# An MoE layer's list stage: SyncE's wait for an add's landing, moved behind the next turning

## The chip, the cores and the metric

The kernel runs on one core of a Trainium2 chip. The metric is the device time of one execution in microseconds (us), the median of the runs. Engines are called PE (TensorE, matmuls; PEld its weight loads), DVE (VectorE), ACT (ScalarE), POOL (GpSimd) and SP (SyncE).

## What is computed

Eight batches of 512 tokens of width 512 pass a cross-attention block and a feed-forward block, each behind a layer norm and with a residual:

```python
x = x + xattn(layernorm(x), ctx_512, Wq, Wkv_expand, Wout)      # 16 heads, 64 context rows
x = x + ffn(layernorm(x), ...)
# ffn, for T = 4096 tokens, E = 8 experts, I = 256:
scores, top_idx = top_k(x @ router_w.T, 2)
comb = zeros((T, E)).at[arange(T)[:, None], top_idx].set(scores)
h = silu(einsum('td,edi->eti', x, wg)) * einsum('td,edi->eti', x, wu)
moe_out = einsum('etd,te->td', einsum('eti,eid->etd', h, wd), comb)
se = silu(x @ sg_w + sg_b) * (x @ su_w + su_b) @ sd_w + sd_b
out = moe_out + se
```

## The kernel before

Tokens are worked in 32 tiles of 128. A first part does attention and the router tile by tile. Then comes one list of 103 entries that share one pipeline: 32 entries of the shared expert, and behind them SLOTS = 71 slots of the routed experts. A slot is up to 128 (token, expert) pairs of one expert; slots are sorted by expert, so there are seven places where the expert changes. "Slot t" below is entry 32 + t, and the change touches only the slots.

What one slot does, engine by engine:

- POOL gathers its token rows from DRAM into one of four buffers (`gather(t)`, line 722, a DMA from POOL's queue), and, much later, adds its result rows onto `out` in DRAM (`add(t)`, line 732, also a DMA of POOL's queue, which accumulates). POOL's own order is gather(t), add(t-6), gather(t+1), add(t-5), and so on.
- PE turns the gathered rows (line 1447, four transposes), one entry later does gate and up (line 1456, 12 matmuls), and two entries after that the down product (line 1456, 6 matmuls that read `hidT`). In one PE entry the order is: transposes of slot t, gate and up of slot t-1, down of slot t-3.
- ACT and DVE form `hid` = silu(gate)*up (lines 925 and 1421), then split it into a high and a low f16 part in `xn2p` (lines 752 and 1385; two buffers). This is "the split activations".
- SP turns the split activations: `turn_hid(t)`, line 517, one DMA transpose from `xn2p` into one of the four buffers of `hidT`. It waits for the split of slot t. PE's down product of slot t waits for its landing. Below this is "turning t".
- DVE scales the down product into one of four buffers of y (line 1436; the tile is named `w_q` in the rows), and POOL's add(t) reads that.

Two adds of different experts can hit the same token, so the add of a slot that begins a new expert must not start before the one ahead of it has landed; within an expert it is enough that the adds up to t-3 have (and by POOL's own wait, t-2). POOL does not decide this itself. SP does, in `pass_turn(t)`: it loads a number that was computed from the routing (line 522), waits until the landed adds have raised their semaphore to it (line 523; the rows show the end of that wait at line 524), and raises `add_turn` (line 524). POOL's add(t) waits for `add_turn` to reach t-2. From slot 3 on there is one such step a slot. As SP runs its list in order, a `turn_hid` that stands behind a waiting `pass_turn` waits too.

```python
def pass_turn(t):
    before_t = sp.value_load(adds_before[0:1, t - 1:t], min_val=16, max_val=16 * SLOTS)
    sp.wait_ge(y_added[(t - 1) % 2], before_t)
    sp.sem_inc(add_turn, 1)

def add(t):                                   # POOL
    pool.wait_ge(y_ready, T + t + 1)
    wait(pool, y_added[t % 2], 16 * (t // 2))
    ...
    wait(pool, add_turn, t - 2)
```

Of the kernel before, what the change touches and what calls it, by code (L numbers as in the profile page):

```python
# [44 lines left out]
SLOTS = 2 * T + E - 1  # L45
# [45 lines left out]
def xattn_moe(nc, x, ctxT, wqT, wkT, wvT, woT, routerT, experts, shared, sh_b, sd_b, out):  # L91
# [5 lines left out]
    with stack:  # L97
# [274 lines left out]
        def _(sp):  # L372
# [141 lines left out]
            def turn_hid(t):  # L514
                sp.wait_ge(parts_ready, t + 1)
                wait(sp, down_mm, T + t - 3)
                sp.dma_start_transpose(hidT[:, t % 4, :, :, :].rearrange("p v c q -> p (v c) q"),
                                       hid_parts[:, t % 2, :, :].rearrange("p v i -> p (v i)")
                                       ).then_inc(hid_turned[t % 4], 16)

            def pass_turn(t):
                before_t = sp.value_load(adds_before[0:1, t - 1:t], min_val=16, max_val=16 * SLOTS)
                sp.wait_ge(y_added[(t - 1) % 2], before_t)
                sp.sem_inc(add_turn, 1)

            for t in range(SLOTS + 1):
                if t < SLOTS - 1:
                    turn_hid(t)
                if t >= 4:
                    pass_turn(t - 1)  # L530


        @block.gpsimd
# [398 lines left out]
        def _(dve):  # L932
# [93 lines left out]
            def low_values(n):  # L1026
                for i, ((rows, dst, src), (_, high, _)) in enumerate(zip(value_parts(1, n), value_parts(0, n))):
                    dve.wait_ge(v_hi, 2 * n + i + 1)
                    low(dst, src, sc[rows, S_V:S_V + 1], high, v_split)
# [718 lines left out]
```

## Time and profile before

| | us |
|---|---|
| median of 3 runs | 790.71 (790.65 to 793.01) |
| the profiled execution, its time | 791.66 |
| its span in the trace | 789.9 |
| PE busy | 760.1 (96%) |
| DVE, ACT, POOL busy | 579.8, 460.0, 433.8 |
| granted TensorE clock, mean | 0.997 |

The span is what the trace covers of one execution; 1.8 us of the execution's time lie around it. PE's busy share says that it is the engine that works nearly all the time. The chain of work that ended last is the place where a wait shows that lengthened the run, and the stretch of the slots begins at about 461 us and ends at 779.7 us, the last down product.

### The profile page before, as it was taken

Reading aid. Unit: us, or ns where it says so; the run is one execution under the profiler, and the core shown is the slowest. Engines: PE = TensorE matmul, PEld = TensorE weight load, DVE = VectorE, ACT = ScalarE, POOL = GpSimd, SP = SyncE. Lnnn points to the kernel's source line nnn. Section 1 sums busy time; section 2 is a strip of 40 time slices with the busy share of each in tenths; the row PEclk is TensorE's granted clock in tenths of the full one; section 3 lists DMA queues with packets and bytes.
Section 4 is the critical chain, followed back from the end, with each engine's and each line's share of the span. In section 5 each row is a group of like instructions: output and inputs, shape, how many; then the busy total and the mean of one; then the engine's idle time right before and its main releaser. Section 6 shows DMA issues by size and latency. Waiting matters only on the chain.

```text
span 789.9 us, 21975 instructions
## 1 busy us (share of the span) xinstructions
PE 760.1 (96%) x7252; PEld 520.8 (66%) x7252; DVE 579.8 (73%) x1199; ACT 460.0 (58%) x847; POOL 433.8 (55%) x563
## 2 busy tenths in 40 slices
PE   5898999999999999999999999999999999999995
PEld 2767888888888887778888864455554545455552
DVE  5999999999989898856898765555555555565552
ACT  4688888998898989775556333333333333333330
POOL 2455787777777777552200203756565565656543
PEclk9999999999999999999999999999999999999998
DMA  8326867777676777778666646989898888979992
GB/s 293 125 78 182 230 192 223 214 211 212 197 217 200 217 220 215 202 221 264 209 201 202 227 137 124 163 136 161 140 156 140 149 144 152 147 134 163 145 148 34
DMA packets 138319, 140.73 MB, mean 178 GB/s; under 512 B 87872, under 2 KB 88896, under 8 KB 137856
## 3 DMA queue, kind: packets, MB, share of 16 engines
q1 hardware_dynamic: 122336, 104.01, 48.6%
q0 software_dynamic: 15904, 35.70, 26.0%
q8 instruction: 47, 0.77, 0.4%
q14 instruction: 32, 0.26, 0.1%
HBM read 71.61 MB, written 52.31 MB: 157 GB/s over the span
## 4 chain that ended last, share of the span: by engine, by line
PE 84%; DVE 7%; DMA 5%; issue 2%; ACT 1%; POOL 0%; SPq 0%; DVEq 0%; POOLq 0%; ACTq 0%
PE psum L1456 45%; PE psum L1525 19%; PE psum L1447 10%; PE psum L1575 5%; DMA hidT<-xn2p 4%; PE psum L1618 3%; DVE kv_store L974 1%; DMA out<-w_q,tabs 1%; DVE head_max L1162 1%; DVE stats L1078 1%; PE psum L1504 1%; DVE probsT L974 1%; DVE w_q L1436 0%; DVE attnT L1132 0%; DVE xn1T L974 0%
## 5 line engine op out<-in xcount | busy, mean ns | idle before, releaser
L732 POOL DMA_INDIRECT out<-w_q,tabs x71 | 112.5, 1584 | 110.7 <-DVE w_q L1436 80.5
L722 POOL DMA_INDIRECT x_in<-normed_tokens,tabs x71 | 71.4, 1006 | 89.9 <-DVE tabs L1315 42.2
L925 ACT ACTIVATE silu_g<-psum,tabs 128x256 f32<-128x256 f32 x71 | 33.6, 473 | 146.0 <-PE psum L1456 143.9
L1421 DVE SCALAR_TENSOR_TENSOR hid<-psum,tabs,silu_g 128x256 f32<-128x256 f32 x71 | 34.3, 484 | 111.2 <-ACT silu_g L925 108.1
L1456 PE MATMUL psum<-exp_all,hidT 128*128 x426 | 103.4, 379 | 3.2 <-DMA hidT<-xn2p 3.2
L1456 PE MATMUL psum<-exp_all,probsT 128*128 x420 | 96.4, 379 | 0.0
L1525 PE MATMUL psum<-xn1T,w_q 128*128 128x128 f16 x1536 | 91.0, 219 | 0.8 <-DVE maxima L957 0.8
L1456 PE MATMUL psum<-w_o,attnT 128*128 128x512 f16 x384 | 88.0, 379 | 1.7 <-DVE attnT L1132 1.3
L1525 PEld LDWEIGHTS psum<-xn1T,w_q 128*128 128x128 f16 x1536 | 86.3, 98 | 2.1 <-issue 2.1
L574 POOL TENSOR_TENSOR exp_all<-piece,exp_all 128x512 f32 (+1 forms) x48 | 56.0, 1166 | 44.5 <-ACT piece L752 44.5
L1456 PEld LDWEIGHTS psum<-exp_all,hidT 128*128 128x128 f16 x426 | 41.7, 98 | 54.2 <-issue 6.2
L1436 DVE TENSOR_SCALAR w_q<-psum,y_w 128x512 f32<-128x512 f32 x71 | 53.3, 751 | 22.1 <-PE psum L1456 17.6
L1456 PEld LDWEIGHTS psum<-exp_all,probsT 128*128 128x128 f16 x420 | 41.1, 98 | 41.9
L1456 PEld LDWEIGHTS psum<-w_o,attnT 128*128 128x128 f16 x384 | 35.1, 97 | 40.9 <-issue 1.6
L752 ACT ACTIVATE probsT<-psum 128x512 f16<-128x512 f32 x99 | 55.6, 600 | 9.0 <-PE psum L1447 8.5
L752 ACT ACTIVATE xn2p<-hid 128x256 f16<-128x256 f32 x70 | 29.2, 417 | 38.6 <-DVE hid L1421 36.4
L1456 PE MATMUL psum<-exp_all,xn1T 128*128 x216 | 49.6, 379 | 0.0
L1456 PE MATMUL psum<-exp_all,qT 128*128 x216 | 49.6, 379 | 0.0
L1575 PE MATMUL psum<-kv_store,qT 128*128 128x256 f16 x384 | 48.5, 273 | 0.2 <-DVE qT L974 0.2
L1456 PE MATMUL psum<-w_sh,hidT 128*128 128x512 f16 x192 | 46.7, 379 | 0.1
L646 POOL TENSOR_TENSOR xn2p<-xn,xn2p 128x512 f16<-128x512 f32 x32 | 37.1, 1159 | 17.4 <-ACT xn2p L752 15.4
L1525 PE MATMUL psum<-probsT,w_sh 128*128 128x128 f16 x768 | 45.5, 219 | 0.0
(216 smaller groups left out, 1652.0 us busy)
## 6 DMA issues: line engine op xcount, KB each, us to landing
x_in<-x SPq DMA_DIRECT2D x64, 256.0 KB, 3.1
exp_all<-experts SPq DMA_DIRECT2D x24, 512.0 KB, 5.2
out<-xy SPq DMA_DIRECT2D x32, 256.0 KB, 3.2
normed_tokens<-xn SPq DMA_DIRECT2D x32, 256.0 KB, 5.2
normed_turned<-xn2T SPq DMA_DIRECT2D x32, 256.0 KB, 3.4
w_q<-out SPq DMA_DIRECT2D x32, 256.0 KB, 2.9
out<-w_q SPq DMA_DIRECT2D x32, 256.0 KB, 2.1
probsT<-normed_turned SPq DMA_DIRECT2D x16, 256.0 KB, 3.5
```

Of the source, the lines that this page charges most:

```text
L574: pool.tensor_tensor(split_piece(e, 1, k), piece[:, :], split_piece(e, 0, k), ALU.subtract).then_inc(piece_split, 1)
L646: pool.tensor_tensor(xn2p[:, 1, :], xn2[:, (j + 1) % 2, 0:H], xn2p[:, 0, :], ALU.subtract).then_inc(xn2_parts, 1)
L722: pool.indirect_dma_start(x_in[:, t % 4, :], None, xn_dram, bass.IndirectOffsetOnAxis(gather_at[:, t:t + 1], 0)).then_inc(gathered[t % 4], 16)
L732: pool.indirect_dma_start(out, bass.IndirectOffsetOnAxis(add_at[:, t:t + 1], 0), y[:, t % Y_RING, :], None, bounds_check=TOKENS - 1, oob_i ...
L752: act.activation(dst, src, ACT.Copy, scale=scale).then_inc(done, 1)
L925: act.activation(silu_g[:, :], psum[:, GU_BANK[m % 2], 0:I], ACT.Silu, scale=gate_scale_at[:, tm:tm + 1]).then_inc(silu_ready, 1)
L1421: dve.scalar_tensor_tensor(hid[:, :], psum[:, GU_BANK[m % 2], I:2 * I], up_scale_at[:, tm:tm + 1], silu_g[:, :], ALU.mult, ALU.mult).then_ ...
L1436: dve.tensor_scalar(y[:, k % Y_RING, :], bank(DOWN_BANK[k % 2]), y_w[:, tk % 4, :], None, ALU.mult).then_inc(y_ready, 1)
L1447: last = pe.transpose(dst[:, c * P:(c + 1) * P], src[:, c * P:(c + 1) * P], ident[:, :])
L1456: last = pe.matmul(dst, lhsT(a, c), rhs(z, c), start=(c == 0 and a == z == 0), stop=(c == n - 1 and a == 1))
L1525: last = pe.matmul(dst[:, o * P:(o + 1) * P], weights(a, c, o), xT[:, z, c, :], start=(c == 0 and a == z == 0), stop=(c == C - 1 and a == 1))
L1575: last = pe.matmul(dst, qT[:, a, c, :], k_bd[:, z, c, :, :].rearrange("p h k -> p (h k)"), start=(a == z == 0 and (j != 2 or c % 2 == 0)), ...
```

## The change

The loop of SP that does both jobs for the slots is run one step longer, and the step that lets an add go is done one turn later. Before, SP's order was turning t, then pass_turn(t-1). Now it is turning t, then pass_turn(t-2).

```diff
-            for t in range(SLOTS + 1):
+            for t in range(SLOTS + 2):
                 if t < SLOTS - 1:
                     turn_hid(t)
-                if t >= 4:
-                    pass_turn(t - 1)
+                if t >= 5:
+                    pass_turn(t - 2)
```

SP's list at the head of the slots, before. L517 is a turning, L522 the load of `adds_before` that opens a pass_turn; a wait for `y_added` belongs to the pass_turn ahead of the row at which it is printed. The five turnings are 0 to 4, the first load is pass_turn(3).

```order
L517 DMA_TRANSPOSE hidT<-xn2p 128x4x128 [waits down_mm,parts_ready,adds_ready]
L517 DMA_TRANSPOSE hidT<-xn2p 128x4x128 [waits down_mm,parts_ready] x4
L522 TENSOR_LOAD adds_before
L522 ISA x2
L517 DMA_TRANSPOSE hidT<-xn2p 128x4x128 [waits y_added0,down_mm,parts_ready]
L522 TENSOR_LOAD adds_before
```

The same place of the changed kernel:

```order
L517 DMA_TRANSPOSE hidT<-xn2p 128x4x128 [waits down_mm,parts_ready] x5
L522 TENSOR_LOAD adds_before
L522 ISA x2
L517 DMA_TRANSPOSE hidT<-xn2p 128x4x128 [waits y_added0,down_mm,parts_ready]
L522 TENSOR_LOAD adds_before
```

One more turning (number 5) stands ahead of the first pass_turn; from there on the two alternate as before, with the slot numbers of pass_turn one lower against those of the turnings.

SP's list at the end of the slots, before. The last turning is number 69; behind it stand pass_turn(68), (69) and (70).

```order
504 L517 DMA_TRANSPOSE hidT<-xn2p 128x4x128 [waits y_added0,down_mm,parts_ready]
505 L522 TENSOR_LOAD adds_before
506 L522 ISA x2
507 L522 TENSOR_LOAD adds_before [waits y_added1]
508 L522 ISA x2
509 L522 TENSOR_LOAD adds_before [waits y_added0]
510 L522 ISA x2
511 L97 UNCONDITIONAL_BRANCH [waits y_added1]
```

And of the changed kernel:

```order
501 L517 DMA_TRANSPOSE hidT<-xn2p 128x4x128 [waits y_added1,down_mm,parts_ready]
502 L522 TENSOR_LOAD adds_before
503 L522 ISA x2
504 L522 TENSOR_LOAD adds_before [waits y_added0]
505 L522 ISA x2
506 L522 TENSOR_LOAD adds_before [waits y_added1]
507 L522 ISA x2
508 L522 TENSOR_LOAD adds_before [waits y_added0]
509 L522 ISA x2
```

Four instead of three pass_turn steps stand behind the last turning, pass_turn(67) to (70). The instructions of PE, DVE, ACT and POOL are the same, in the same order.

## Rows read from the trace of the kernel before

**Rows 1.** The page: the chain that ended last by engine.

```profile
PE 84%; DVE 7%; DMA 5%; issue 2%; ACT 1%; POOL 0%; SPq 0%; DVEq 0%; POOLq 0%; ACTq 0%
```

**Rows 2.** The waits, 395 to 790 us: waiter, releaser; us, times, longest.

```profile
PE psum L1456 <- DMA hidT<-xn2p: 3.2, 5, 1.0
SPq L524 <- DMA out<-w_q,tabs: 22.8, 8, 3.9
```

**Rows 3.** The chain in order of time, same stretch: start us, us, what.

```profile
502.15 0.44 PE psum L1447 x4
...
592.91 0.44 PE psum L1447 x4
...
598.38 7.07 DMA hidT<-xn2p
...
674.35 6.55 DMA hidT<-xn2p
...
769.03 0.44 PE psum L1447 x4
```

**Rows 4.** The timeline, 559 to 575 us: start us, us, engine line [idle before <-releaser].

```profile
561.97 0.99 POOL L722 DMA_INDIRECT x_in<-normed_tokens,tabs  x1 [0.30 <-issue]
...
563.37 0.41 DVE L1385 TENSOR_TENSOR xn2p<-hid,xn2p 128x256 f16<-128x256 f32 x1
...
564.28 1.59 POOL L732 DMA_INDIRECT out<-w_q,tabs  x1 [1.32 <-DVE w_q L1436]
...
569.84 1.46 PE L1456 MATMUL psum<-exp_all,hidT 128*128 x6
...
571.14 0.60 PE L1447 MATMUL psum<-ident,x_in 128*128 128x128 f32 x4
```

**Rows 5.** SP by line, ns min/median/max, first and last start: 517, then 524 from 563 us.

```profile
L517 SPq DMA_TRANSPOSE hidT<-xn2p x70: 1189/1190/2506, 475.4 to 774.5; - x70
...
L524 SPq EVENT_SEMAPHORE  x1: 17/17/17, 565.8 to 565.8; - x1
```

**Rows 6.** An expert's change, 590 to 606 us: POOL's timeline, SP's line 524, PE.

```profile
590.21 1.59 POOL L732 DMA_INDIRECT out<-w_q,tabs  x1 [1.44 <-DVE w_q L1436]
...
596.27 1.59 POOL L732 DMA_INDIRECT out<-w_q,tabs  x1 [3.19 <-SPq L524]
...
599.51 1.59 POOL L732 DMA_INDIRECT out<-w_q,tabs  x1 [0.30 <-issue]
...
L524 SPq EVENT_SEMAPHORE  x1: 17/17/17, 595.3 to 595.3; - x1
```

**Rows 7.** DMA queues, 559.49 to 561.6 us: packets, MB, share of 16 engines.

```profile
q1 hardware_dynamic: 544, 0.13, 30.8%
```

**Rows 8.** The same, 598.38 to 600.4 us.

```profile
q0 software_dynamic: 130, 0.25, 103.7%
q1 hardware_dynamic: 18, 0.00, 1.2%
```

**Rows 9.** The same, 498.46 to 503.3 us.

```profile
q1 hardware_dynamic: 544, 0.13, 26.2%
```

**Rows 10.** The timeline, 486 to 503 us.

```profile
495.93 0.99 POOL L722 DMA_INDIRECT x_in<-normed_tokens,tabs  x1 [0.30 <-SPq L524]
497.22 1.59 POOL L732 DMA_INDIRECT out<-w_q,tabs  x1 [0.30 <-issue]
498.02 0.41 DVE L1385 TENSOR_TENSOR xn2p<-hid,xn2p 128x256 f16<-128x256 f32 x1
499.11 0.99 POOL L722 DMA_INDIRECT x_in<-normed_tokens,tabs  x1 [0.30 <-issue]
```

**Rows 11.** The end: the chain, and POOL's timeline from 764 us.

```profile
774.92 6.59 DMA out<-w_q,tabs x2
...
778.81 1.55 POOL L732 DMA_INDIRECT out<-w_q,tabs  x1 [2.33 <-DMA out<-w_q,tabs]
...
782.52 1.55 POOL L732 DMA_INDIRECT out<-w_q,tabs  x1 [0.30 <-issue]
```

## The prediction

> **What bounds the kernel now.** Start with the chain that ended last [rows 1]: 84% of it is PE, so the run is PE working without a break, and only what makes PE wait or what comes behind PE's last product can move the time. The second view is the chain in order of time for the slots [rows 3]. Slot 9's transposes start at 502.15 us and slot 30's at 592.91, so 21 slots took 90.76 us, or 4.322 each. From slot 30 to slot 70 (769.03) it is 176.12 us for 40 slots, where 40 x 4.322 = 172.87. **3.25 us** were lost there. The chain names the place: three pieces "DMA hidT<-xn2p" of 6.5 to 7.07 us, of which the rows show the first and the last, are turnings that landed after PE wanted them, and the waits list five such waits, 3.2 us in all [rows 2]. The rest of the 3.25 us follows directly behind each, as PE catches up with the engines it feeds. One of the five is at the start of the slots and outside the stretch.
>
> The third view is one undisturbed slot [rows 4]. DVE ends the split of slot 21 at 563.78 and SP issues turning 21 at once (563.81). Its down product starts at 569.84. A turning has thus **6.03 us** to land: two periods, 8.64 us, less 2.61. How much it needs is seen in the DMA queues. A turning is 544 packets of queue 1, and for turning 20 all 544 lie within 2.1 us of the issue [rows 7].
>
> Why was turning 29 late, which was issued on time at 598.38? SP waited for the landing of add 25 (issued 590.21, released at 595.3, so 5.1 us) before it could issue turning 28, and let add 26 go only then, at 596.27 instead of some 594.5 [rows 6]. Turning 28 had slack for its 1.4 us. But add 26, the gather behind it and add 27 (599.51) now sat on the DMA engines at the wrong moment: in the first 2.0 us of turning 29, queue 0 filled the engines (103.7%) and only 18 of the 544 packets moved [rows 8]. So what costs PE time is not SP's wait as such, but **where an add's transfer lies against a turning**. SP's waits for adds were 22.8 us in 8 pieces [rows 2] and cost PE 3.25.
>
> **The change, step by step.**
>
> *In every slot, SP's step comes later.* SP reaches line 524 some 2.0 us after it issued the turning (563.81 to 565.8), 1.19 of them the issue itself [rows 5], and POOL's add starts 1.0 us behind line 524 (595.3 to 596.27, [rows 6]). Before, add t was let go behind turning t+1, long ahead of its data: add 19 waited only for DVE and started at 564.28, that is 0.5 us behind turning 21 [rows 4]. Now add t is let go behind turning t+2, so it starts at 2.0 + 1.0 = 2.9 to 3.0 us behind turning t+2. Every add, and with it every gather in POOL's order, moves **2.4 us** later within a period of 4.32. The add then stands 1.4 us ahead of the next turning, where it stood 3.8 ahead.
>
> *At a change of expert, SP no longer holds a turning back.* Add t-1 starts 2.9 behind turning t+1 and lands 5.1 later, which is 3.7 behind turning t+2. The next turning is due at 4.32. SP waits some 1.7 us in idle time. The three late pieces should go: **-3.25 us**, taken whole. If an add needs over 5.8 us, part of this stays.
>
> *Turnings against the shifted adds.* This is the unknown. The best row is at the start of the slots, where the queue happened to stand nearly as it will in every slot: turning 6 was issued at 498.43 (the end of its split), with an add 1.2 us ahead (497.22) and a gather 0.7 behind (499.11) [rows 10]. After the change the figures are 1.4 ahead and 0.5 behind. All 544 packets were through within 4.8 us [rows 9], against 2.1 for turning 20, and PE was not held up by it. With 6.03 us to land in, that holds, with about 1 us to spare. The row at the other side is turning 29, with its add 2.1 ahead: 7.07 us, too late. Bounds: nothing from turning 6; from the 6.55 us of the milder late piece in [rows 3], a period of (6.55 + 2.61) / 2 = 4.58, so 0.26 us on some 62 slots, **+16 us**. I take **+1.0**, three or four late landings of some 0.3 us, as 1.4 is nearer to 1.2 than to 2.1. It can't be below nothing, as PE has no other gap.
>
> The Trainium skill, in "DMA: Bandwidth & Descriptors", section "Queues, rings and completion order", says that each DMA engine round-robins between its queue rows packet by packet. By that rule a turning should get its share while an add runs, and a shifted add would cost it little: the term above would be 0 and the sum 1.0 us lower. [Rows 8] speak against leaning on it here, with 18 packets of one queue beside 130 of the other.
>
> *Gathers come later.* Gather 25 starts at 561.97 and its transposes at 571.14, 9.2 us behind [rows 4]; 2.4 less leaves 6.8. At a change the add is released by a landing at 3.7, starts at 4.6 to 4.7 instead of 2.9, and takes the gather behind it along: 5.1 us are left. No row gives a gather's landing. The shortest margin that the trace shows is gather 9, 495.93 [rows 10], with transposes at 502.15 [rows 3]: 6.2 us, and PE did not wait. So the ordinary slots are covered by 0.6, and the changes are not shown to be. Bounds: 0, and 5 changes x 1.5 = 7.5 us, if a gather needs the 6.55 of the slowest turnings. I take 0.2 at each of the five changes whose add lands slowly, **+1.0**.
>
> *The y buffers* (four) are no limit: add t-4 starts 2.9 us behind turning t-2 and lands 5.1 later, at 8.0; DVE writes the y of slot t some 14.7 behind it at the earliest (two periods and 6.03 to the down product).
>
> *The end.* The last turning (69) is issued at 774.5 [rows 5]. Behind it, before, only pass_turn(68) to (70) stand, which hold nothing up: add 67 goes at 774.92 with its data, add 68 at 778.81, add 70 at 782.52 [rows 11]. Now pass_turn(67) stands there too, so add 67 starts at 774.5 + 3.0 = 777.5, 2.6 us later. Add 69 must wait for its landing, by POOL's own wait; an add took 5.1 us in traffic, and at the end add 68 took 2.7 (778.81 to the end of the chain's piece at 781.51). With 4.2 between them, add 69 may start at 777.5 + 4.2 + 1.0 = 782.7 and add 70 one instruction and gap (1.55 + 0.3) later, at 784.6: **+2.1 us**, and nothing hides it, since PE is done by then. With 2.7 for the landing it is +0.6, with 5.1 it is +3.0.
>
> *Sum* against the profiled execution's 791.66: -3.25 + 1.0 + 1.0 + 2.1 = +0.85, so 792.5. The median is 0.95 below the profiled execution, which gives **791.6**.
>
> **The rivals.**
>
> *A. The shifted adds make turnings late all the time: slower.* The mechanism is that of turning 29, in every slot. It decides at 6.03 us between a turning's issue and its landing. For it: an add 2.1 us ahead cost 7.07, turning 6 had only about 1 us of slack, and a stalled PE widens the period, which moves the add from 1.4 ahead towards 2.1. Against it: turning 6, and that no second add follows closely, as add 27 did. A third of the 16 us is 5.3 us; with the other terms (-3.25 + 1.0 + 2.1) that is +5.2, and the median **796**. Two late gathers of over 1 us have the same sign.
>
> *B. The gain without the costs: faster.* Turnings and gathers all land in time and the end costs only its lower bound: -3.25 + 0.6 = -2.65, **788.1**. For it: the three late pieces are a clear loss, and the tail's price hangs on one landing. It needs everything at its lower end.
>
> *C. The change does not take the wait away.* If adds at the changes take 6 us in the new traffic, SP still holds turnings back, and half of the 3.25 us stays: **793.2**. In sign it lies with the forecast or with A.
>
> **How the numbers follow.** About 0.3%, 2.4 us, is what a measurement of this kernel can tell from no change. The forecast (both small terms together under 2.5 us) has 0.48, A has 0.34, B 0.08, C 0.10, of which 0.02 lie inside 2.4 us. So faster 0.08, same 0.50, slower 0.42. The range reaches down to 788.8, into B, and up to 798.5, past A's 796 but far from the 16 us bound.
>
> **What the new profile would show.** POOL's adds (line 732) each wait for SP's line 524 and start 2.9 us behind a turning. The waits of SPq L524 for "DMA out" are then short and no turning starts late. The three late pieces of 6.5 us and more are gone from the chain, and transposes come every 4.32 us. Where A holds, "DMA hidT<-xn2p" stands in the chain slot after slot, and the period is above 4.32. Where gathers are late, PE's line 1447 waits for "DMA x_in" a few slots behind each change. The last add starts some 15.6 us behind slot 70's transposes, not 13.5 (769.03 to 782.52). The prediction is wrong if the period changes at all outside the changes of expert, or if the end does not move.

## The result and the profile after

The changed kernel takes **798.71 us** (median of 6 runs, 798.28 to 800.96), the kernel before beside it 791.12 us (6 runs, 790.52 to 793.12). The ratio is 1.0097, with a 95% interval of 1.0076 to 1.0117: slower by 7.6 us. The forecast was 791.6, "same"; the range ended at 798.5, just below the measured time. Ratios here and below leave out four executions that stand far above the others of their kernel (805.14 us with the old end, 2046.42 with the gathers ahead, 816.91 and 818.97 with known turns). The profiled execution took 798.28 us with a span of 796.6; that of before took 791.66.

First the page of the changed kernel: the chain by engine (before: [rows 1]), and POOL's adds, whose columns are busy us, mean ns, idle before them and what ended most of it.

```profile
PE 81%; DVE 6%; issue 4%; DMA 4%; SPq 2%; ACT 1%; POOL 1%; POOLq 0%; DVEq 0%; ACTq 0%
...
L732 POOL DMA_INDIRECT out<-w_q,tabs x71 | 112.8, 1589 | 115.9 <-SPq L524 77.5
```

PE's share fell from 84 to 81%: PE waits more. Next the waits behind 395 us (waiter, releaser; us, times, longest), to be set beside [rows 2]:

```profile
POOL out L732 <- SPq L524: 77.5, 41, 3.3
POOL out L732 <- DVE w_q L1436: 18.8, 7, 3.7
PEld psum L1456 <- issue: 7.5, 8, 2.1
PEld psum L1447 <- issue: 4.2, 8, 0.8
PE psum L1456 <- DMA hidT<-xn2p: 4.1, 3, 1.9
PEld psum L1447 <- DMA x_in<-normed_tokens,tabs: 3.9, 5, 1.7
PE psum L1447 <- DMA x_in<-normed_tokens,tabs: 1.8, 2, 1.2
```

and SP's own wait in the same stretch:

```profile
SPq L524 <- DMA out<-w_q,tabs: 13.8, 9, 2.9
```

The adds now wait for SP, as the change intends. SP's waits for adds shrank from 22.8 to 13.8 us. Waits of the transposes (line 1447) for gathers, "DMA x_in", are new against the first trace of before. Then the chain in order of time (start us, us, what), to be set beside [rows 3] and [rows 11]; slot 9's transposes are at 504.87 and slot 30's at 596.82:

```profile
491.01 7.47 DMA hidT<-xn2p
...
504.87 0.44 PE psum L1447 x4
...
596.82 0.63 PE psum L1447 x4
...
640.58 4.78 DMA x_in<-normed_tokens,tabs
...
679.93 6.29 DMA x_in<-normed_tokens,tabs
...
773.77 0.44 PE psum L1447 x4
...
779.24 1.19 SPq L517
...
782.53 4.83 DMA out<-w_q,tabs x2
787.74 1.42 issue
789.15 1.55 POOL out L732
```

The three late turnings between slots 30 and 70 are gone from the chain. Two late gathers stand there instead, and the end is another. PE's transposes cut the executions into stretches. The columns are us; "slot 0" is where its transposes start, "product 70" is the start of slot 70's down product, and "again" is the second trace of the same kernel, from the experiments below:

| kernel | slot 0 at | slots 0 to 9 | 9 to 30 | 30 to 70 | slot 70 to product 70 | to the end |
|---|---|---|---|---|---|---|
| before | 460.94 | 41.05 | 90.75 | 176.12 | 9.79 | 11.28 |
| after | 462.76 | 41.95 | 92.11 | 176.79 | 11.80 | 11.15 |
| difference | +1.82 | +0.90 | +1.36 | +0.67 | +2.01 | -0.13 |
| before, again | 463.51 | 40.18 | 90.81 | 174.25 | 9.79 | 11.28 |
| after, again | 461.74 | 41.70 | 92.06 | 176.38 | 11.40 | 11.44 |

The 1.82 us ahead of the slots, where the change touches nothing, are chance: over all kernels of this study slot 0 starts between 460.3 and 463.5 us, and in the second pair of traces it is the kernel before that starts later. One piece of it may be a stretch of 3.4 us from 24.4 us at a granted clock of 0.5 (1.2 GHz; PE had been busy for 2.6 of the 4.4 us ahead of it), which the first execution of before didn't have and the second did. From slot 0 on the changed kernel is 4.8 us longer in the first pair of traces and 6.7 in the second.

Does the adds' shift have the size that was predicted? POOL's timeline shows an ordinary slot (start us, us, engine line, operation, [idle before <- releaser]); the turning of the slot was issued at 668.93:

```profile
668.93 18.49 SPq L517 DMA_TRANSPOSE hidT<-xn2p  x5
...
669.74 0.99 POOL L722 DMA_INDIRECT x_in<-normed_tokens,tabs  x1 [0.31 <-issue]
...
672.30 1.59 POOL L732 DMA_INDIRECT out<-w_q,tabs  x1 [1.57 <-SPq L524]
...
676.26 0.60 PE L1447 MATMUL psum<-ident,x_in 128*128 128x128 f32 x4
```

The add starts 3.4 us behind the turning, which is also the median over adds 10 to 64, where 2.9 to 3.0 was predicted. The gather has 6.5 us to its transposes (median; before 9.3).

### The profile page after: what moved, and what is told of

It reads as the page before. It is cut to its first block, busy times and chain, and to the rows that moved or that the text cites. A ratio compares the mean times of both kernels' runs of the same rounds, so it can differ in the third digit from the quotient of the medians.

```text
span 796.6 us, 21975 instructions
## 1 busy us (share of the span) xinstructions
PE 761.9 (96%) x7252; PEld 520.6 (65%) x7252; DVE 580.4 (73%) x1199; ACT 460.1 (58%) x847; POOL 432.9 (54%) x563
## 4 chain that ended last, share of the span: by engine, by line
PE 81%; DVE 6%; issue 4%; DMA 4%; SPq 2%; ACT 1%; POOL 1%; POOLq 0%; DVEq 0%; ACTq 0%
PE psum L1456 42%; PE psum L1525 19%; PE psum L1447 10%; PE psum L1575 5%; PE psum L1618 3%; DMA x_in<-normed_tokens,tabs 1%; DMA out<-w_q,tabs 1%; DMA hidT<-xn2p 1%; DVE kv_store L974 1%; SPq L517 1%; SPq L522 1%; DVE head_max L1162 1%; DVE stats L1078 1%; POOL out L732 1%; DVE probsT L974 0%
## 5 line engine op out<-in xcount | busy, mean ns | idle before, releaser
L1447 PEld LDWEIGHTS psum<-ident,x_in 128*128 128x128 f32 x284 | 34.7, 141 | 19.4 <-issue 4.2
```

The source lines that it names most:

```text
L1447: last = pe.transpose(dst[:, c * P:(c + 1) * P], src[:, c * P:(c + 1) * P], ident[:, :])
```

## The experiments

All ratios are to the kernel before, measured side by side with each set of kernels, with 95% intervals; a hundredth of a per cent is 0.08 us. Where two ratios are subtracted, the interval of the difference is worked out from the two (as the root of the sum of squares).

**How far do two measurements of one kernel agree?** Both kernels were run again, unchanged.

> The changed kernel once more, for a second trace of it. In the first one, 1.8 us of the 6.6 us between the two traces lay ahead of the slots, where the change has no instruction. If that part is an accident of one execution, the slots begin within 0.5 us of 460.9 us here, and the time is still 7 us or so above before, which the slots must then carry alone. If it belongs to the change (SP's code is one instruction shorter, so code is fetched elsewhere), they begin at 462.8 again. Theory G (gathers late at the changes of expert): PE's transposes of slots 33, 41, 50, 58 and 66 wait again, as 33, 41, 50 and 58 did (0.2, 0.7, 1.4, 0.1 us). If these move to other slots, the causes are accidents of the DMA traffic.

Measured: 796.53 us, ratio 1.0073 (1.0049 to 1.0097). So the loss is 5.8 to 7.7 us. The slots begin at 461.74 us, between the two values named. Of the transposes that had waited for a gather, those of slots 33 and 58 wait again (0.1 and 1.1 us), those of 41 and 50 do not, and those of 67 are new (0.6). All of them stand seven or eight slots behind a change of expert, so the place is the change's and the size of each wait is chance.

> The kernel before once more, for a second trace. Its 28 runs lay between 787.9 and 793.9 us with a median of 790.3, and the first trace is of a run of 791.7 us. If the three late turnings (3.25 us between slot 30 and slot 70) were bad luck of that one execution, this trace loses under 2 us there, and the forecast's gain was never worth 3.25 us. If they are the rule, it is 3 us again. The ratio is 1.000 within 0.002 either way, which shows what the timing can tell.

Measured: 791.48 us, ratio 1.0005 (0.9985 to 1.0025). Its chain, in order of time, two DMA pieces of the slots:

```profile
497.33 6.31 DMA x_in<-normed_tokens,tabs
...
708.41 7.02 DMA hidT<-xn2p
```

One late turning, not three: slots 30 to 70 took 174.25 us, so 1.38 were lost there and not 3.25. How many turnings are late differs from one execution to the next, and a gather was late in the kernel before too (0.6 us of PE's wait). The two traces of before are of one length all the same (789.9 and 789.8 us): the second begins its slots 2.6 us later.

**Does the late step at the changes of expert bring the gain?** The order of before, and only the seven steps that held SP come a turn later:

```diff
+            CHANGES = (9, 18, 26, 34, 43, 51, 59)
 ...
-                if t >= 4:
+                if t - 2 in CHANGES:
+                    pass_turn(t - 2)
+                if t >= 4 and t - 1 not in CHANGES:
                     pass_turn(t - 1)
```

> Before's order, but at the seven changes of expert (slots 9, 18, 26, 34, 43, 51, 59, written in as numbers, which only fits this routing) the step that waits for the landing stands one turning later, together with the next slot's. So SP no longer holds a turning back, and no ordinary add moves. Theory S (SP's hold on the turnings is what cost before its 3.25 us): the late turnings 29, 37 and 46 are gone, 3 us faster than before, ratio 0.996. Theory P (what costs is where an add's transfer lies against a turning, here adds 26 and 27 close to each other): adds 26, 34, 43 are released by the same landing at the same time, turnings 29, 37, 46 are as late as before, ratio 1.000 within 0.002.

Measured: 790.16 us, ratio 0.999 (0.9972 to 1.0008). In its trace the mechanism is as predicted. SP's own waits:

```profile
SPq L524 <- DMA out<-w_q,tabs: 1.5, 1, 1.5
```

None of the three turnings is late; slots 30 to 70 took 173.36 us, 0.49 above 40 x 4.322. But in time it is worth 0.8 us, within noise of nothing, and the 0.996 of theory S lies outside the interval.

**What do the late gathers cost?** In POOL's list each gather goes one add earlier, first in the changed kernel, then in the kernel before:

```diff
-ADD_BEHIND = 6
+ADD_BEHIND = 7
```

> The changed kernel with POOL's adds one step further behind its gathers (seven instead of six), so each gather is issued one period earlier, ahead of the add that SP now delays. Theory G (gathers late): no transposes wait for a gather, which gives back 2.4 us in the changed kernel's trace, ratio 1.0067 or better. Theory T (turnings late because the shifted adds sit on them): the adds stay at 2.9 us behind a turning, so late turnings stay and the ratio is near 1.0097. The gather now lies elsewhere against the turning (some 2 us ahead of the add instead of behind it), so turnings may land at another time, and that too tells which of the two transfers delays them.

Measured: 792.76 us, ratio 1.0026 (1.001 to 1.0043), 0.47% below the changed kernel measured beside it. There is no wait for "DMA x_in" left, and the adds still start 3.4 us behind the turnings.

> The kernel before with POOL's adds one step further behind the gathers, nothing else. In the changed kernel the same edit took 3.7 us off: 1.8 us between slot 0 and slot 9, 2.0 us between slot 30 and slot 70. If both come from gathers that were late, before has only the first to win (its gathers had 9.3 us): 1 to 1.8 us, ratio 0.998. If the edit helps because it takes a gather out of the stretch in which a turning lands, before's late turnings 29, 37 and 46 shrink too, and it is 3 to 4 us faster, ratio 0.9955.

Measured: 789.74 us, ratio 0.9981 (0.9967 to 0.9994). Turnings 29, 37 and 46 are not late in its trace (none of the 70 needs over 5.7 us), yet the gain is that of the smaller forecast. So the earlier gathers bring 3.7 us (0.47%) in the changed kernel and 1.5 us (0.19%) in that of before. The difference, **2.2 us**, is what the late gathers that are due to the change should cost. By the ratios alone it is uncertain (plus or minus 2.5), and the edit does more than one thing: in the kernel before it also moves the adds, from 3.85 to 1.85 us ahead of a turning. But the traces of the changed kernel give the same size: the slots that are longer because their transposes waited for a gather lose 2.4 us in the first and 2.3 in the second.

**What does the end cost?** The changed kernel, with before's order from turning 65 on:

```diff
-            for t in range(SLOTS + 2):
+            for t in range(SLOTS + 1):
 ...
-                if t >= 5:
+                if 5 <= t <= 65:
                     pass_turn(t - 2)
+                if t >= 65:
+                    pass_turn(t - 1)
```

> The changed kernel, but from slot 65 on SP is back in before's order (one turning with two steps behind it, then each step behind its own turning). In the trace of the changed kernel PE's last down products lost 2.0 us (8.8 us from that of slot 67 to that of slot 70, 6.8 before), as turning 69 landed 4.8 us after its issue, not 2.5. If the shifted adds do this, turning 69 lands within 2.6 us here, the last four products take 6.8 us, and the kernel is 2.0 us faster than the changed one, ratio 1.007 to before. If it is an accident of that one execution, the ratio stays at 1.0097. By the forecast's own step, in which the chain of the last adds costs 2.1 us, the gain would be there too, but in the distance from the last product to the end.

Measured: 795.30 us, ratio 1.0052 (1.0031 to 1.0073), 1.7 us (0.21%) below the changed kernel measured beside it, which alone is within the noise. The same kernel once more:

> The changed kernel with SP's old order from slot 65 on, again, since its first trace was of a disturbed execution. The ratio was 1.0052 against 1.0073 for the changed kernel. If the shifted add makes the last turning late, that turning lands within 2.6 us here, against 4.75 us, and PE's stretch from slot 70's transposes to its down product is 9.8 us, against 11.8 and 11.4. The ratio is 1.005 again.

Measured: 795.39 us, ratio 1.0049 (1.003 to 1.0069). From slot 70 to product 70 it takes 9.79 us, and 11.28 to the end, as before. This execution also shows how much late gathers can cost in a single one. From its waits (the transposes' line is 1449 here) and its chain:

```profile
PEld psum L1449 <- DMA x_in<-normed_tokens,tabs: 7.7, 5, 2.3
```

```profile
602.22 5.48 DMA x_in<-normed_tokens,tabs
...
637.56 5.95 DMA x_in<-normed_tokens,tabs
...
677.97 6.39 DMA x_in<-normed_tokens,tabs
...
715.42 6.55 DMA x_in<-normed_tokens,tabs
```

All four stand behind a change of expert, 35 to 40 us apart, where the changed kernel's trace leaves only 4.6 to 4.9 us between gather and transposes. Its slots 30 to 70 took 180.73 us.

Then both cures at once, the earlier gathers and the old end:

> The changed kernel with both edits, the gathers one step ahead and SP's old order from slot 65 on. If the two costs are separate places that add up, it is at 1.0026 less 0.0022, ratio 1.0004 within 0.002: then late gathers and the end make up the whole loss of the change, and the adds' later place against the turnings costs PE nothing more than SP's hold did before. If the ratio stays at 1.002 to 1.003, the end is not a place of its own, and late turnings cost 2 us beyond what they did before.

Measured: 791.96 us, ratio 1.0001 (0.9985 to 1.0017). Against the kernel with the earlier gathers alone that is 0.25% less (plus or minus 0.23), so the end is worth **2.0 us**. Three comparisons give 1.7 to 2.0, and the traces show 2.0 and 1.6 between slot 70 and product 70.

**Does the start matter?** In the changed kernel turning 4 landed 7.47 us behind its issue (first row of the chain above), in that of before 6.53. Here the steps up to turning 10 are those of before:

```diff
-                if t >= 5:
+                if 4 <= t <= 10:
+                    pass_turn(t - 1)
+                if t >= 12:
                     pass_turn(t - 2)
```

> The changed kernel, but SP keeps before's order up to turning 10 (each step behind the next slot's turning) and goes over to the later one behind turning 12. Slot 0 to slot 9 took 41.05 and 40.18 us in the two traces of before, 41.95 and 41.70 in the two of the changed kernel. Theory St (the change costs about 1 us at the start, where adds 2 to 5 are let go late and gathers 9 to 11 with them): the stretch is at 40.2 to 41.1 here and the kernel 1 us faster than the changed one, ratio 1.006. If the start is chance, nothing moves: 1.0073.

Measured: 797.88 us, ratio 1.0096 (1.006 to 1.0131). Slots 0 to 9 took 40.06 us, but slots 9 to 30 took 93.90, and nothing arrives in the time. The interval is nearly 3 us to either side and touches 1.006, so a cost of 1 us at the start is neither shown nor excluded.

**Is it the position of the add that makes a turning late?** SP's step is shorter if it doesn't read its count from the table but waits for a constant, which is right for this routing alone. The shifted adds then start 2.2 us behind a turning, some 1.2 earlier than in the changed kernel:

```diff
-                before_t = sp.value_load(adds_before[0:1, t - 1:t], min_val=16, max_val=16 * SLOTS)
-                sp.wait_ge(y_added[(t - 1) % 2], before_t)
+                sp.wait_ge(y_added[(t - 1) % 2], 16 * ((t - 1) // 2 + (t in (9, 18, 26, 34, 43, 51, 59))))
```

> The changed kernel in which SP knows the numbers that it otherwise loads (written in, which fits this routing alone). The load and its checks are gone, so line 524 comes 1.2 us behind a turning's issue, not 2.0, and adds and gathers start 0.8 us earlier in every slot: an add 2.2 us ahead of the next turning, not 1.0 to 1.4. Theory D (the later adds and gathers go, the worse: gathers late, end late): about a third of the 2.9 us of shift is taken back, ratio near 1.005. Theory T (the place against the turning, by which 2.1 us ahead was the worst seen): turnings need 6 us and more in most slots, PE waits for them slot after slot, ratio 1.012 or more.

Measured: 811.72 us over six executions and 808.8 over the four that the ratio counts, ratio 1.0222 (1.0175 to 1.0269). One load and its checks less on SP, and the kernel loses another 1.3 to 1.5%. The waits (PE's line is 1455 here), and four of the eleven turnings that stand in the chain behind slot 9:

```profile
PE psum L1455 <- DMA hidT<-xn2p: 16.8, 17, 2.4
```

```profile
543.50 6.91 DMA hidT<-xn2p
...
557.59 7.53 DMA hidT<-xn2p
...
572.19 8.49 DMA hidT<-xn2p
...
666.27 6.97 DMA hidT<-xn2p
```

This is rival A's picture. But in this kernel the gather too had moved: it is now issued 0.2 to 0.4 us ahead of the turning. To tell the two apart, the same kernel with ADD_BEHIND 7, in which the adds nearly stay and the gathers go elsewhere:

> The kernel with the numbers written in (adds 2.2 us ahead of a turning, ratio 1.022, 17 waits of PE for a turning) and the gathers one step ahead, which moves the gather from between the add and the turning to ahead of the add. It tells which transfer delays a turning. If the add alone does, the late turnings stay and the ratio is 1.015 to 1.022. If it is the gather whose transfer begins while the turning's packets run (it was issued 0.3 to 0.4 us ahead of the turning), they shrink, turnings land within 6 us, and the ratio is 1.005 or below.

Measured: 790.07 us, ratio 0.9991 (0.9979 to 1.0003). The adds stand nearly where they stood (1.8 us ahead of a turning, against 2.1), the gathers 3.1 ahead and 1.2 behind.

```profile
PE psum L1455 <- DMA hidT<-xn2p: 1.2, 2, 0.8
```

So an add some 2 us ahead of a turning does not make it late by itself. What nearly all turnings of 6.5 us and more have in common is a **gather issued just ahead of them**, behind that add. The DMA queues show it (packets, MB, share of 16 engines) in the 3.13 us behind turning 42's issue, first with the gather 0.2 ahead, then with the gathers moved:

```profile
q0 software_dynamic: 191, 0.42, 109.9%
q1 hardware_dynamic: 378, 0.09, 14.7%
```

```profile
q0 software_dynamic: 155, 0.31, 74.4%
q1 hardware_dynamic: 543, 0.13, 19.6%
```

In the second kernel the turning's packets begin 1.9 us behind its issue and all but one are through at 3.13. In the first they begin at 1.6, but at 3.13 us 360 of the 544 have moved (18 of the 378 are the last ones of turning 41), the rest comes in between the gather's, and the turning landed 6.97 us behind its issue (the last of the rows above).

The same is true of the kernel before, and it answers the question that the prediction asked of turning 29. The row between adds 26 and 27 in the timeline of [rows 6] is a gather, and turning 29 was issued at 598.38:

```profile
598.16 1.04 POOL L722 DMA_INDIRECT x_in<-normed_tokens,tabs  x1 [0.30 <-DVE w_q L1436]
```

All turnings of 6.5 us or more in the two traces of before (4, 29, 37 and 46; 54) had a gather 0.1 to 0.4 us ahead and its add 2.0 to 2.3 ahead. Over 13 of the 14 traces (not that of the 805.14 us execution), 56 turnings stand like this, most of them in the kernel with known turns: half need over 6.5 us, as far as their landings are recorded. Of 150 turnings with an add at the same place (1.7 to 2.2 ahead) but the gather 3 us or more ahead, half need under 3.7, and none over 6.03. A gather just ahead without its add, two us before it, was not tried, as POOL issues the two in a row.

The Trainium skill ("DMA: Bandwidth & Descriptors", "Queues, rings and completion order") has each engine take turns between its queue rows and drain a whole packet of descriptors from one before it switches. No run here tests that: what the traces count as packets need not be these. And what looks like a turning held at nothing is mostly its issue. In those traces no turning has a packet in the first 1.17 us, also where nothing else was in its way, so [rows 8] tell of 0.85 us and not of 2.0: there 18 packets of the turning moved beside some 80 of the other queue, and in the next 1.0 us 391 beside 30.

**Is there a better kernel?** The seven late steps of the second experiment and the earlier gathers together, with the table read as before:

> Before's order with both things that gained something: gathers one step ahead (ratio 0.9981) and the step of a change of expert one turning later (0.999). If they are separate, 0.997. If the gathers ahead already took the late turnings away, SP's hold has nothing left to cost, and it stays at 0.998.

Measured: **788.00 us** (786.87 to 788.68), ratio 0.9962 (0.9949 to 0.9974), the fastest of all and faster than both kernels. Slots 30 to 70 took 172.87 us, 40 x 4.322 to the last digit. Its seven numbers fit this routing only; ADD_BEHIND 7 alone, which fits any, gives 0.9981.

**Where do the steps in all slots cost, once gathers and end are cured?** The fastest kernel and the one with both cures differ, apart from the last few steps, in one thing: whether the step is late at the seven changes or in all slots. With it the adds stand 1.0 us ahead of a turning and not 1.8, while the gathers stand at the same places. That is 0.9962 against 1.0001, **3.1 us** (plus or minus 1.6). In the trace with both cures the loss lies in eight slots, 21, 33, 41, 50, 54, 58, 62 and 66, which are 0.2 to 0.7 us longer than 4.322, 3.8 us in all. In the fastest kernel's trace no slot behind 9 is. The waits, first both cures, then the fastest kernel:

```profile
PEld psum L1449 <- issue: 5.4, 10, 0.9
PEld psum L1458 <- issue: 4.8, 9, 1.3
PE psum L1458 <- DMA hidT<-xn2p: 1.4, 3, 0.8
```

```profile
PEld psum L1459 <- issue: 1.5, 2, 1.2
PEld psum L1450 <- issue: 0.7, 3, 0.3
```

Most of it is "issue", for which the profile names no cause. Two pieces of the chain with both cures name one, turnings 55 and 59:

```profile
712.79 6.28 DMA hidT<-xn2p
...
730.70 6.26 DMA hidT<-xn2p
```

PE does a slot's down product three entries later, so these are the long slots 58 and 62. The other six fit the same way: turnings 18, 30, 38, 47, 51 and 63 landed 5.7 to 6.1 us behind their issue, about the 6.03 that they have, and their down products start at most 0.2 us late. All eight are the turning of a change's own slot or the fourth behind it. What comes late is what PE's sequencer (the part that hands PE its instructions) does behind its wait for the turning. It has to load the number of the next expert from a table before it can go on to the next transposes. In slot 41 with both cures turning 38 landed at 643.5. The load's line (as above: ns, first and last start), then two rows of the chain, idle time and the next transposes:

```profile
L1649 PEldq TENSOR_LOAD <-expert_of x1: 1065/1065/1065, 644.1 to 644.1; - x1
...
645.30 0.30 issue
645.59 0.63 PE psum L1449 x4
```

The same slot in the fastest kernel, where turning 38 landed 4.4 us behind its issue: a load just as slow starts 2.4 us ahead of the next transposes, and costs nothing.

```profile
L1650 PEldq TENSOR_LOAD <-expert_of x1: 982/982/982, 642.1 to 642.1; - x1
...
644.51 0.60 PE L1450 MATMUL psum<-ident,x_in 128*128 128x128 f32 x4
```

The load is usually short. In the changed kernel, by line (ns min/median/max, first and last start):

```profile
L1647 PEldq TENSOR_LOAD <-expert_of x71: 296/313/1257, 465.3 to 775.2; - x71
```

It starts 0.52 us behind the landing at the earliest, and transposes that wait for it follow its end by some 0.54. They are due 1.30 us behind the down product's start, that is 7.33 behind the turning's issue. So, by an estimate from these numbers, a turning has 6.0 us with a load of 0.3 us, and 5.3 with one of 1.0. The fastest kernel has more loads above 600 ns (25 of 71, against 18), and pays nothing, as no turning behind slot 9 needs over 5.5 us.

This holds for the 13 traces as a whole. They have 86 slots behind slot 9 that are over 0.06 us longer than 4.322. In 19 the next transposes start within 0.1 us of their gather's landing. In the other 67 they start 0.45 to 0.61 us behind the end of such a load, where the median slot of a trace has 1.3 to 3.0 us. So the "issue" time ahead of PE's transposes is late turnings too (in four of the 67 slots, those of before's order with the gathers ahead, turnings that SP issued late).

## Why the prediction was wrong

The terms, each a difference of ratios, in us of 791, with what the prediction had for it:

| term | predicted | measured |
|---|---|---|
| late turnings at the changes, taken away | -3.25 | -0.8 (alone) to -1.5 (0.9962 against 0.9981), each plus or minus 1.4 |
| turnings against the shifted adds | +1.0 | +3.1, plus or minus 1.6 |
| gathers | +1.0 | +2.2, plus or minus 2.5; in two traces 2.4 and 2.3 |
| end | +2.1 | +2.0, plus or minus 1.8; in two traces 2.0 and 1.6 |

The measured terms add up to +5.8 to +6.5, and measured were +5.8 and +7.7. The agreement with +5.8 is no check of the terms: they are steps on one way from the kernel before to the changed one, so they must add up to its ratio.

- **The late turnings at the changes, -3.25: a step that failed by its size.** That SP's hold made turnings late is right, and the seven late steps alone take that away. How it did is not quite as said: the hold moved the gather behind the held add to 0.1 to 0.4 us ahead of the next turning, and the prediction weighed the adds. The size came from one execution. Three late turnings there are one, costing 1.38 us, in the second. A loss that differs so from one execution to the next is read from more than one, or is put at its mean. 2 us of the miss are here.
- **Turnings against the shifted adds, +1.0: the margin was wrong.** Turnings did land later (median 4.45 us behind their issue, against 3.25), and a few at the changes and behind them at 5.7 to 6.3. The prediction gave them 6.03 us, to the start of the down product. It left out what PE's sequencer does behind that wait, the load of the next expert's number, which brings the margin down to 5.3 us when the load takes 1.0. It expected three or four late landings of 0.3 us; with gathers and end cured there are eight, of 0.2 to 0.7. Another 2 us of the miss. It also took turning 6's last packet, 4.8 us behind the issue, for its landing; the trace has the landing at 5.3. And of the 2.0 us in [rows 8] no turning has a packet in the first 1.17. Rival A had the mechanism, late turnings by the shifted add, and a price near the measured one (796). That price was partly luck: it had the turnings at a third of 16 us, 5.3, and they are 3.1, in 8 of some 60 slots and not slot after slot. Its picture appears only in the kernel with known turns, where the gather comes just ahead of the turning.
- **The gathers, +1.0: the place right, the size half.** Transposes wait behind changes of expert, as said. The margin there was 4.6 to 4.9 us (predicted 5.1), and landings reached 6.3 and 6.55 us, so a late one costs 1.5 and not 0.2. The upper bound, 5 x 1.5, had been worked out with 6.55 us too, borrowed from a turning; the value was taken at its low end without a row for a gather's landing. Median landings were 4.6 us, in the kernel before too.
- **The end, +2.1: right.** Add 70 starts 15.4 us behind slot 70's transposes (773.77 to 789.15; before 13.49), the prediction said 15.6, and the chain goes as predicted through add 67 (782.53) and its landing after 4.83 us. It wasn't the only way: turning 69 too landed late, 4.75 us behind its issue against 2.47, and held the last product back by 2.0 us. Its y was ready at 787.67, 1.5 us ahead of add 70, nearly as close as before (1.6), so curing the adds alone would probably have gained little; it was not tried.
- **Rival C** fell in part: SP's waits did not vanish (13.8 us), yet none made a turning late enough to stand in the chain behind slot 9. **Rival B** fell by all three costs. The sign of being wrong that the prediction named, a period that changes outside the changes of expert, came true in part: with both cures the long slots are the third and the seventh behind a change, and the others keep 4.32.

The signs of all four terms were right, and the end's size. Two costs at their low ends beside a gain at its full size made "same" of a loss.

## What to carry to other kernels

A step that is moved in every round of a loop is priced by everything that is queued behind it: here the adds were aimed at, and the gathers behind them and the last round paid. Where a margin shrinks from 9 to 5 us and no row says what the transfer needs, take the slowest transfer that the trace shows. A margin ends not where the waiting engine starts again but where the work behind it in its sequencer is no longer late: here that took 0.7 us off 6.03. And before an order is changed to save a wait, try giving the reads behind it one place more of lead: that alone made this kernel 0.2% faster.

## What the runs showed of the hardware

- How long a transposing DMA of 544 packets takes depends on which transfers start beside it. Its last data packet starts 2.8 us behind the issue (median of turnings 10 to 64) in the kernel before, 3.2 with the adds 1.8 ahead and the gathers 3.1 ahead and 1.2 behind, and 4.15 with the add 2.1 and the gather 0.4 ahead. The last two kernels take 790.1 and 808.8 us. A load and its checks taken off SP put the gathers into the bad place.
- No turning has a packet in the first 1.17 us behind its issue (910 turnings in 13 traces); the issue itself takes 1.19 us.
- A load of one number by PE's sequencer takes 0.30 us at the least (the median is 0.30 to 0.36 in all kernels but one), and 0.9 to 1.3 us at times, in every kernel here. It costs PE time only where it starts late: 67 of the 86 long slots end with one.
- One kernel's executions differ by some 3 us to either side (787.89 to 793.93 us over 28 runs of the kernel before). The traces show two parts of it: the number of late turnings changes (3.25 and 1.38 us between slots 30 and 70), and so does the time at which the slots begin (460.3 to 463.5 us). What is read from one trace is known no better than that.
